# A fused cross-attention and FFN kernel on one core: another opening, and a product of Q between the two heads' products with V in every pair

## The reference, cut to what matters

```
x   = x + xattn(layernorm(x), ctx, mask, bias, Wq, Wk, Wv, Wo)     # x, ctx: 16 x 64 x 512, 32 heads of 128
x   = x + ffn(layernorm(x), base_W, router_W, A, B, ...)
xattn: q = hq @ Wq; k = hkv @ Wk; v = hkv @ Wv
       score = q k^T / sqrt(128) + bias; p = softmax(where(mask, score, -inf)); out = (p v) @ Wo
ffn:   base = x @ base_W^T + b; w = top 8 of 15 router probabilities, mapped to 8 experts
       out = base + 2 * sum over experts of w_e * (x A_e^T) B_e^T
```

## Time and profile before

| what | value |
|---|---|
| median of 3 runs | 777.95 us (777.52 to 778.46) |
| profiled execution | 777.37 us |
| its span | 775.5 us |
| PE busy | 766.0 us (99%), 6272 matmuls |
| PE weight loads | 639.1 us (82%), 6272 |
| DVE, ACT, POOL busy | 541.8, 384.8, 196.6 us |
| granted TensorE clock | 0.999 over the span |
| DMA | 133.05 MB, mean 172 GB/s |

### The profile page before, as it was taken

How to read it: one execution, slowest core, us unless ns; L and a number is a source line. 1 busy time by engine, 2 the same in 40 slices (tenths; PEclk the granted TensorE clock), 3 DMA queues, 4 the chain that set the end, 5 groups by cost and what they waited for, 6 DMA issues and landing times.

```text
span 775.5 us, 16682 instructions
## 1 busy us (share of the span) xinstructions
PE 766.0 (99%) x6272; PEld 639.1 (82%) x6272; DVE 541.8 (70%) x979; ACT 384.8 (50%) x1110; POOL 196.6 (25%) x203
## 2 busy tenths in 40 slices
PE   9999999999999999999999999999999999999998
PEld 7888888888888888887888888888888888888886
DVE  5874626257677676578778877887678767867974
ACT  5662526245555464475654465435543565426510
POOL 0224041014424433323132312232122313010300
PEclk9999999999999999999999999999999999999999
DMA  6536673244565456577766777556756666541002
GB/s 231 203 123 217 220 244 137 109 140 160 163 190 164 164 163 187 167 235 217 229 181 209 226 208 208 170 176 205 201 165 197 201 188 196 154 148 57 1 15 95
DMA packets 128236, 133.05 MB, mean 172 GB/s; under 512 B 46479, under 2 KB 93583, under 8 KB 128158
## 3 DMA queue, kind: packets, MB, share of 16 engines
q1 hardware_dynamic: 128158, 132.00, 54.3%
HBM read 88.98 MB, written 42.99 MB: 170 GB/s over the span
## 4 chain that ended last, share of the span: by engine, by line
PE 94%; DVE 3%; issue 1%; ACT 1%; DMA 0%; ACTq 0%
PE pY L1452 43%; PE pP L1452 40%; PE pY L1613 4%; PE pO L1649 2%; PE pT_ L1649 1%; PE pO L1452 1%; DVE y L1167 1%; ACT pr L798 1%; PE pS L1649 1%; DVE st L1018 1%; PE pO L1501 0%; PE pS L1501 0%; DVE wk_lo L948 0%; PE pY L1528 0%; DVE wo_lo L948 0%
## 5 line engine op out<-in xcount | busy, mean ns | idle before, releaser
L798 ACT ACTIVATE pr<-pr,mx 128x64 f32<-128x64 f32 x256 | 86.2, 343 | 68.0 <-DVE mx L1187 68.0
L1452 PE MATMUL pY<-wo_hi,oT_hi 128*128 128x512 f32 x248 | 97.3, 392 | 0.3 <-DVE y L1167 0.2
L1452 PE MATMUL pY<-wo_lo,oT_hi 128*128 128x512 f32 x248 | 96.6, 389 | 0.0
L1452 PE MATMUL pY<-wo_hi,oT_lo 128*128 128x512 f32 x248 | 96.5, 389 | 0.0
L1167 DVE TENSOR_TENSOR y<-y,pY 128x512 f32<-128x512 f32 x124 | 83.9, 676 | 15.2 <-PE pY L1452 14.1
L690 ACT CAST wk_hi<-twk 128x256 fp32r<-128x256 f32 x128 | 50.7, 408 | 65.2 <-PE pP L1452 53.4
L948 DVE TENSOR_TENSOR wk_lo<-wk_raw,wk_hi 128x256 fp32r<-128x256 f32 x96 | 48.5, 506 | 46.5 <-ACT wk_hi L690 45.1
L1452 PE MATMUL pP<-xo_hi,wk_hi 128*128 128x512 f32 x196 | 77.9, 398 | 0.0
L1452 PE MATMUL pP<-xo_lo,wk_hi 128*128 128x512 f32 x196 | 76.4, 390 | 0.0
L1452 PE MATMUL pP<-xo_hi,wk_lo 128*128 128x512 f32 x196 | 76.4, 390 | 0.0
L623 POOL TENSOR_TENSOR bias<-bias,madd 128x512 f32<-128x512 f32 x32 | 41.3, 1306 | 137.6 <-DMA bias<-in_fside_Bx32xSxS 137.5
(11 more groups left out here) (283 smaller groups left out, 1862.2 us busy)
## 6 DMA issues: line engine op xcount, KB each, us to landing
v_hbm<-stage SPq DMA_DIRECT2D x64, 256.0 KB, 2.1
k_hbm<-stage SPq DMA_DIRECT2D x64, 256.0 KB, 3.7
k<-k_hbm SPq DMA_DIRECT2D x16, 1024.0 KB, 6.4
v<-v_hbm SPq DMA_DIRECT2D x16, 1024.0 KB, 7.2
wk_raw<-in_L_xattn_Wk SPq DMA_DIRECT2D x16, 512.0 KB, 4.6
wo_raw<-in_L_xattn_Wo SPq DMA_DIRECT2D x16, 512.0 KB, 3.7
bias<-in_fside_Bx32xSxS SPq DMA_DIRECT2D x128, 64.0 KB, 3.6
wk_raw<-in_L_xattn_Wq SPq DMA_DIRECT2D x16, 512.0 KB, 4.6
```

The source lines that it names most:

```text
L798: nc.scalar.activation(pr[s][:, b, :], pr[s][:, b, :], ACT.Exp, bias=mx[:, s, b:b + 1], accum_out=sm[:, s, b:b + 1]).then_inc(exp_made, 1)
L1452: mm = nc.tensor.matmul(bank_, a, b, start=first and n == 0, stop=last and n == len(terms) - 1, skip_group_check=read_between)
```

## The change

Four things are changed, each in the written order.

1. Opening, TensorE: of the 26 small warm-up transposes 8 are left. The four matmuls of the first product that need only high parts of the weight (`with_high`) are issued ahead of `turn_ctx(1)`, the two that need the low part (`with_low`) behind it.
2. Opening, ACT: the cast of weight slot 5 stands behind the casts of tile 4's transpose.
3. Opening, DVE: `first_t3` stands behind the low parts of tile 4; `first_low(2)` stands ahead of `first_t1` and `first_t4`.
4. Attention: in every pair i from 0 to 13 the first of the pair's remaining products of Q (`times(n, 1)`, in pair 0 `times(n, 2)`) stands between `times_v(2i)` and `times_v(2i+1)`, not behind both.

```diff
@@ ACT @@
-            higher(0, 5)
             last_high(0)
             act.wait_ge(turned, SECOND_TURN[0] + 1)
             nc.scalar.copy(a21[0][:, :, :], ...).then_inc(a21_h, 1)
+            higher(0, 5)
             rows_out(1)
@@ DVE @@
             lower(b12[1][:, :, :], raw_block(0, 0, 1), b12[0][:, :, :], b12_l)
-            first_t3()
 
             dve.wait_ge(a21_h, 1)
             last_low(0)
             lower(a21[1][:, :, :], ...)
+            first_t3()
             first_t2()
...
             make_c11(1)
+            first_low(2)
             first_t1()
             first_t4()
-            first_low(2)
@@ PE, opening @@
+            def with_high(bank_, pairs):
+                for n, (a, b) in enumerate((a[i], b[0]) for a, b in pairs for i in range(2)):
+                    nc.tensor.matmul(bank_, a, b, start=n == 0, stop=False)
+
+            def with_low(bank_, pairs):
+                for a, b in pairs:
+                    nc.tensor.matmul(bank_, a[0], b[1], start=False, stop=False)
...
-            warm_up(26, 32)
+            warm_up(8, 32)
+
+            pe.wait_ge(a01_lo, 1)
+            pe.wait_ge(w_hi[0], 1)
+            with_high(pP[0][:, :], of_slots(0, 0, 0))
             turn_ctx(1, first_turn(1))
-
             pe.wait_ge(w_lo[0], 1)
-            pe.wait_ge(a01_lo, 1)
-            product(pP[0][:, :], of_slots(0, 0, 0), last=False)
+            with_low(pP[0][:, :], of_slots(0, 0, 0))
             times(1, 1)
@@ PE, pairs 0 to 13 @@
                 times_v(h)
+                products = [1, 2, 6, 7] if i else [2, 6, 7]
+
+                times(n, products.pop(0))
                 times_v(h + 1)
-                for p in (1, 2, 6, 7) if i else (2, 6, 7):
+                for p in products:
                     times(n, p)
```

## The result

| what | before | after |
|---|---|---|
| median of 12 runs | 777.85 us (776.19 to 779.76) | 781.04 us (779.27 to 782.10) |
| ratio of the timed runs | | 1.0038, 95% interval 1.0028 to 1.0048 |
| profiled execution, span | 777.37, 775.5 us | 781.68, 779.8 us |
| start of pair 0's products with V | 346.65 us | 348.22 us (+1.57) |
| from there to the start of pair 14's | 349.84 us | 352.55 us (+2.70) |

The account below looks back on a forecast made before the run. TensorE, busy 766.0 of 775.5 us, bounds the kernel. Stalls -5.5, seams +4.3, late work +0.2, opening +0.3 give -0.7, taken as -1.0 from the median 777.95: 776.9 us, range 774.8 to 780.0.

Parts of the forecast that it names:

- The stalls are late packets: In the odd head's products with V, pairs 3, 4, 7, 8, 11: TensorE waits for its next instruction packet, 5.5 us.
- the block taken as 3.9 us long: Packet late in pairs 4 and 8: after the change its block lasts 3.9 us, above the 3.13 to 3.73 needed.
- The first bound: Lower bound of the stalls' gain: 4.0 us if packets with only 0.2 us to spare are late now and then.
- The rival without packets: Stalls in the pairs are not packets and stay, only the cost is added: +4.8, 782.7 us; chance 0.06.
- So I take all five stalls as gone: 5.5 us less: Pairs 3, 4, 7, 8, 11: moved packets come in time, 5.5 us gained, bounds 4.0 and 5.9.
- 0.3 of their spread: Varying packet lateness raises the median, so -1.0 was taken from the median where the profiled execution's sum was -0.7.
- Net +0.31 us per pair: Cost of TensorE's extra shape changes around the product between the heads: 0.31 us in 14 pairs, 4.3 us.
- the first rival: Cheaper seams, more stall removed: V behind a large product costs 0.20, all 5.9 us go; 775.0 us, chance 0.22.
- I put 0.2 in all, between 0 and 1: Waits from ACT and DVE running later in the pairs, pairs like 5 waiting 0.1 to 0.2: 0.2 us in all.
- The second rival: copy_p1 becomes the wait at product 6 in 13 pairs from 1 on: 3.9 us, 780.9 us; chance 0.13.
- The order on ACT and DVE otherwise moves work within slack: Opening: apart from tile 4's earlier low parts, the new ACT and DVE order moves work within slack.
- The other term, TensorE's part: Opening: tile 1's transposes and product 1 start about 0.4 us later; opening +0.3 us, between -0.3 and +0.6.

Follow-up runs that it names:

- e5: Kernel before, with the product of Q between the heads only in pairs 3, 4, 7, 8 and 11, copy_p1 ahead of the cast there: 775.22 us, ratio 0.9977.
- e9: As the kernel with the product between the heads in only five pairs (3, 4, 7, 8, 11), with pair 12 added: 774.81 us, ratio 0.9978 to before.
- e8: Kernel before, with only the moves of higher(0, 5) on ACT and first_t3 on DVE, first_low(2) not moved: 777.20 us, ratio 1.0003.
- e2: Kernel before, with only the loop's change (product between the heads in pairs 0 to 13), old opening: 778.05 us, ratio 1.0016.
- e3: Changed kernel, with first_low(2) on DVE back behind first_t1 and first_t4: 778.81 us, ratio 1.0028 to the kernel before.
- e4: Changed kernel, with copy_p1 on ACT ahead of the cast of head two's first bank in pairs 1 to 13: 779.04 us, ratio 1.0031 to before.
- e11: Changed kernel, with add_tile 0 on DVE ahead of the low part of weight slot 1 in every pair: 779.18 us, ratio 1.0031 to before.
- e7: Kernel before, with only TensorE's part of the new opening (8 warm-ups, four high-part matmuls ahead of turn_ctx(1)): 779.56 us, ratio 1.0034.

## Why the prediction was wrong

**The stalls are late packets: right.** All five went, as computed from a count. The counts above, the multiples of 256 and the landings of the packets confirm it with other work in the same places. The one remainder, 0.33 us in pair 4, came in the block taken as 3.9 us long, 1.46 us after its packet had landed. The first bound, 4.0 of 5.9, allowed for that. The rival without packets is refuted. The Trainium skill, "Runtime: NRT & Kernel Launch", section Instruction fetch mechanics, gives TensorE room for 2048 instructions, refilled in blocks of 256, and calls the cost of crossing into the next block mostly hidden. The blocks agree with the runs. The rest does not: with that much room, 128 pairs of load and matmul could not run TensorE dry, and it did run dry, for up to 2.26 us.

**What the stalls are worth: too large.** The step "So I take all five stalls as gone: 5.5 us less" is true of the one profiled execution, and the forecast even added 0.3 of their spread. e5 and e9 gained 1.8 and 1.7 us net of seams of 2.0 and 2.3, so a usual run loses some 4 us to them. By the lengths of the stalls e8, with before's loop, lost 3.1 in the same five pairs, where before lost 5.0, and 0.6 in pair 12. One trace was taken for the typical one.

**The seams: mis-sized.** "Net +0.31 us per pair" measured 0.39 in e2, e3 and e4 and 0.44 in the changed kernel and e11; what the other 0.05 is stays open. The single seams were right (0.15, 0.34, 0.32). Two small terms were missing. Head two's 64 loads and matmuls take 0.94 us when they start afresh and 0.90 when they follow head one. And the product between the heads takes 1.59 us from its start to head two's, not 1.24 + 0.32, since its matmuls follow each other 0.228 to 0.236 apart. 14 x 0.39 is 5.5 us, not 4.3. Against it the first rival is refuted: 0.32 stands in the trace, not 0.20. The Trainium skill, "TensorEngine Tiling (Array Packing)", Key Properties, says that a change of tiling mode drains the engine; the 0.32 here, against 0.23 between large matmuls, fits with that.

**What becomes late: mis-sized.** "I put 0.2 in all, between 0 and 1" was 2.1 us in the profile, 0.83 of it in pair 0, beside the 0.33 of the packet. The chain was the named one (ACT later, DVE's low part, add_tile, times_wo 2), and the earlier trace rows showed 0.06 to spare. What was not carried through is that the 0.65 us by which ACT is late use up that spare in every pair where DVE's low part meets POOL's mask add: six pairs in this execution, fewer in e2 and e3. How much of it a usual run pays stays open: e4 and e11, which remove it, are each 0.5 us faster by the ratios, within their intervals. The second rival named this end (780.9) by another mechanism, a wait for copy_p1, and no run shows that one: its number is luck.

**The opening: failed.** "The order on ACT and DVE otherwise moves work within slack" is the sentence. The new order of first_low(2) was not followed to what it waits for, and costs 0.8 to 1.0 us (e3). The other term, TensorE's part, is some 0.4 by the profiles, near the 0.3 forecast. That product 1 came at 10.00, with 10.1 forecast, says less: it came at 9.26 to 10.21 in seven traces with the old opening and at 9.54 to 10.31 in six with the new. By the ratios the opening costs 1.7 us on top of the loop (1.0038 against 1.0016), where 0.3 stood; the profiles account for 1.2 of it. On the old loop it costs 3.4. That there it also moves the stalls is seen; that this makes up the difference is argued, not shown.

**The sum anew, for a usual run.** Stalls -3.7, seams 14 x 0.39 = +5.5, late adds +0.5, opening +1.7: +4.0, against 3.0 measured (2.2 to 3.7). All but the seams rest on ratios, each uncertain by 0.7 us or more. The excess is in the loop: e2 measured +1.2 (0.5 to 2.0), where -3.7 and +5.5 give 1.8 and its waits for y 0.4 more. The seams are read to 0.02 us, so it is the worth of the stalls in a usual run that is known least; it may be nearer 4.5. That rest stays open.

## What to carry to other kernels

A change that is made in every round of a loop must be weighed against what it cures in a few: here 0.39 us in fourteen pairs against about 0.8 us in five, and the same move in only the pairs that stall is 0.2% faster. Before an instruction is moved ahead on an in-order engine, look up when its input lands, for all behind it waits with it. Take an intermittent stall's worth from several executions, and expect it to move when the count of instructions ahead of it changes.

## What the runs showed of the hardware

- TensorE can run out of instructions where loads and matmuls are small. There were 31 stalls of 0.13 to 2.26 us in eight kernels. The view names nothing but "issue", but all stand at a count of instructions 193 above a multiple of 256, and all end 1.21 to 1.52 us after a packet of 256 instructions has landed. 36 instructions less at the start of the program moved them to other pairs; that kernel is 2.6 us slower (e7), 0.4 of it in the opening.
- DVE's subtraction of 128x256 took 0.42 us, 1.28 while POOL did an add of 128x512 (after, pair 0) and up to 1.47 (before, pair 4); one of 128x16 went from 0.18 to 0.98.
- From 64x64 tiles to a large matmul and back: 0.15 us from the last small one to the first large, 0.34 in place of 0.23 from that to the next, 0.32 to the first small one again, and 64 small pairs that take 0.94 us in place of 0.90.
